# Context products in float32 on two 64-column halves, and maxima in pairs on two 64-row halves

## The reference

```python
q_big = einsum('bshk,hkq->bshq', hidden_q @ Wq.T, w_kc_q)   # then rope, width 192
kv_r  = rope(kv_c)                                          # [b, 1444, 64]
q_r, k_r = einsum(q_big, W_qr), einsum(kv_r, W_kr)          # width 64
attn  = softmax(einsum('bhsr,bhlr->bhsl', q_r, k_r))
ctx_c = einsum('bhsl,bld->bhsd', attn, kv_r)                # then w_kc_kv and Wo
```

## Time and profile before

| | |
|---|---|
| median of 3 runs | 2277.09 us (2274.82 to 2286.96) |
| the profiled execution | 2283.25 us, span 2281.4 us |
| weights and queries | to 305 us |
| first attention | 308 to 1373 us |
| the rest | to the end |
| mean granted clock of TensorE | 0.905 of full speed |

### The profile page before, as it was taken

The page is one execution under the profiler, slowest core; times in us unless marked ns, Lnnn a source line. Parts: engine busy times, 40 slices in busy tenths (PEclk is TensorE's granted clock), DMA queues, the critical chain, the costliest instruction groups (busy, mean ns, idle before and its releaser), DMA issues. The chain is left out here.

```text
span 2281.4 us, 38538 instructions
## 1 busy us (share of the span) xinstructions
PE 1857.9 (81%) x10550; PEld 1632.6 (72%) x10550; DVE 1492.1 (65%) x2799; ACT 1220.5 (53%) x2996; POOL 1117.1 (49%) x961
## 2 busy tenths in 40 slices
PE   4999958999999999999999973499993689837870
PEld 3677736888888888888888963499993466626870
DVE  4677777777777777767776433377774466656763
ACT  2111115777777767767777851366661266515650
POOL 0455528888788888878888852300004100014005
PEclk9999967999999999999999985699996599958985
DMA  5522251111111111111110002455542100026654
GB/s 159 197 58 57 55 176 55 63 63 63 45 54 63 64 31 63 63 64 63 63 54 11 16 8 78 140 197 196 204 165 58 34 1 0 0 77 196 198 164 113
DMA packets 115748, 195.76 MB, mean 86 GB/s; under 512 B 48213, under 2 KB 94265, under 8 KB 110161
## 3 DMA queue, kind: packets, MB, share of 16 engines
q1 hardware_dynamic: 107409, 180.88, 24.6%
q0 software_dynamic: 8192, 13.15, 2.0%
HBM read 147.01 MB, written 46.63 MB: 85 GB/s over the span
## 5 line engine op out<-in xcount | busy, mean ns | idle before, releaser
L501 POOL TENSOR_TENSOR EL<-E,EH 128x400 fp32r<-128x400 f32 x688 | 833.4, 1239 | 158.5 <-ACT EH L733 154.0
L599 DVE TENSOR_REDUCE PM<-bank 128x1 f32<-128x482 f32 (+1 forms) x624 | 397.2, 650 | 185.9 <-PE bank L578 182.9
L742 ACT ACTIVATE E<-bank 128x400 f32<-128x400 f32 x768 | 386.4, 503 | 212.8 <-PE bank L793 153.2
L733 ACT ACTIVATE EH<-E 128x400 fp32r<-128x400 f32 x768 | 407.0, 532 | 0.0
L175 PE MATMUL bank<-EH,KVH 128*128 128x400 f32 x768 | 283.1, 369 | 19.8 <-POOL EL L501 18.5
L578 PE MATMUL bank<-KH,QS 128*128 128x482 f32 (+1 forms) x624 | 250.9, 414 | 53.9 <-DVE KVL L549 27.6
L1248 POOL DMA_INDIRECT m_back<-rows_out,m_slots x64 | 64.8, 1013 | 450.8 <-DMA rows_out<-m_ys 421.2
L792 PE MATMUL bank<-QS,KH 128*128 128x400 f32 x768 | 272.1, 354 | 14.9 <-issue 9.1
L793 PE MATMUL bank<-QB,KB 66*128 66x400 f32 x768 | 269.1, 350 | 0.0
L175 PE MATMUL bank<-EH,KVL 128*128 128x400 f32 x768 | 265.7, 346 | 0.0
L175 PE MATMUL bank<-EL,KVH 128*128 128x400 f32 x768 | 265.5, 346 | 0.0
(11 more groups left out here) (244 smaller groups left out, 3983.3 us busy)
## 6 DMA issues: line engine op xcount, KB each, us to landing
m_stage_u<-in_m_up SPq DMA_DIRECT2D x20, 1392.0 KB
raw<-in_ctx_T SPq DMA_DIRECT2D x16, 1444.0 KB, 6.1
m_xg<-rows_in SPq DMA_DIRECT2D x55, 256.0 KB, 4.1
rows_out<-m_ys SPq DMA_DIRECT2D x55, 256.0 KB, 3.7
m_stage_d<-in_m_down SPq DMA_DIRECT2D x20, 696.0 KB
queries<-q_out SPq DMA_DIRECT2D x64, 200.0 KB, 2.4
QS<-queries SPq DMA_DIRECT2D x16, 800.0 KB, 6.1
rows_in<-zeros SPq DMA_DIRECT2D x5, 1792.0 KB
```

Source lines behind the costliest of these rows:

```text
L501: ops.tensor_tensor(EL[:, n % PB, :], E[:, n % EB, :], as_f32(EH[:, n % PB, :]), ALU.subtract).then_inc(sem, 1)
L599: nc.vector.tensor_reduce(PM[:, f:f + 1], psum[F0 + f % f_banks(b)][:, 0:KW[f % KC]], AX.X, ALU.max).then_inc(red_done, 1)
L733: nc.scalar.activation(EH[:, n % PB, :], E[:, n % EB, :], ACT.Copy).then_inc(hi_done, 1)
L742: nc.scalar.activation(E[:, n % EB, :], psum[S0 + n % SB][:, 0:CH], ACT.Exp).then_inc(exp_done, 1)
```

## The change

The context products use the exponentials in float32 as they are. EH, EL, KVH, KVL and the steps that make them go; the rotated keys are kept once, as KV (float32, `[P, KT, DC]`). A batch has 24 steps, each with one key tile and two score tiles of 4 heads: the even heads of eight (o = 0) and the odd ones (o = 1). The two context products of a step write rows 0 to 63 and 64 to 127 of one bank, CTX.

The row sums leave TensorE's long sums: VectorE adds the even heads' exponentials up in a PSUM bank, ACC (`sum_even`), GpSimd the odd heads' in EA (`sum_odd`), and after 12 steps a product with `ones` per half adds over the partitions (`sums`). GpSimd also takes the first ten parts of the rotation from VectorE.

QB now has 128 rows: the maximum in rows 1 and 2, a row for the padded keys in row 0, the high part of the queries in rows 64 to 127. The maximum uses the high part of the queries alone. Its 39 pieces go in 20 pairs, the even piece with rows 0 to 63 of QS and KH, the odd one with rows 64 to 127 of QB and KH, into two banks that one reduction reads. The list of TensorE has 12 double steps: pair, scores of two steps, pair, context products of two earlier steps.

In `latent_queries` M2 has 64 columns. Two heads' narrow products write the halves of one bank, and high and low part are made for both heads at once into `out_h` and `out_l`, which SyncE sends in four transfers. At the start VectorE clears more: QB over rows 64 to 127 (pad) and 0 to 63, KB over rows 0 to 63, then rows of ones and PAD one by one, and the first query loads wait for that. SR and RS take two transfers each.

Added lines and some unchanged ones (what is removed is in the kernel above):

```diff
...
+                    nc.tensor.matmul(psum[2 + h % 2][0:HALF, half * DC:(half + 1) * DC],
+                                     wqr[:, h, half * HALF:(half + 1) * HALF], wkr[:, h, :], start=True, stop=True)
...
+                def narrow(c, j):
+                    pe.wait_ge(rot_done, c * H + (BUFS + 2 * j + 2))
+                    pe.wait_ge(lo_done, c * HP + (j + 1))
                     for half in range(2):
+                        for o in range(2):
+                            h = 2 * j + o
+                            last = nc.tensor.matmul(psum[4 + j % 2][o * DC:(o + 1) * DC, 0:CH], M2[:, half, h, :],
+                                                    rot[:, h % TURNS, half, :], start=half == 0, stop=half == 1)
...
+    NS = 2 * KT
+    KC, KW = 3, 482
+    KAT = [0, 481, SK - KW]
     NF = QT * KC
+    NP = -(-NF // 2)
     SB, FB = 3, 2
+    EB = 8
...
+    PAD = -1.0e30
+    S0, F0, CTX, ACC, MISC = 0, 3, 5, 6, 7
+    SUM_AT, SUM0_AT, OUT_AT, TURN_AT = 2, 8, 9, 10
+    RECIP_AT, CT_AT = 9, 14
+    ROT_AT = (3, 4, 5, 6, 8, 9, 10, 11, 13, 14)
+    HI_AT, LO_AT = (17, 18), (18, 20)
+    ROT = 11
...
+        KV = [fixed(ctx, nc, f"KV{r}", [P, KT, DC]) for r in range(BUFS)]
...
+        R = fixed(ctx, nc, "R", [P, EB, 2, CH])
+        EA = fixed(ctx, nc, "EA", [P, CH])
+        ES = fixed(ctx, nc, "ES", [P, 2, 2, CH])
+        ones = fixed(ctx, nc, "ones", [P, DC])
...
+        def max_pair(pe, b, i):
             r = b_mod(b)
+            depth = 2 if b is FIRST else 1
+            if i >= depth:
+                pe.wait_ge(red_done, b_val(b) * NP + (i - depth + 1))
             elif b is not FIRST:
+                pe.wait_ge(red_done, b_val(b) * NP)
+            for f in pieces(i):
+                t, j = divmod(f, KC)
+                rows = slice((f % 2) * DC, (f % 2 + 1) * DC)
+                high = QB if f % 2 else QS
+                last = nc.tensor.matmul(psum[f_bank(b, i) + f % 2][:, 0:KW], high[r][rows, t * P:(t + 1) * P],
+                                        KH[r][rows, KAT[j]:KAT[j] + KW], start=True, stop=True)
+            last.then_inc(f_ready, 1)
...
+        def reduce_pair(v, b, i):
+            v.wait_ge(f_ready, b_val(b) * NP + (i + 1))
+            if i == 0 and b is not FIRST:
                 v.wait_ge(nm_ready, b_val(b))
+            k, n = f_bank(b, i), len(pieces(i))
+            nc.vector.tensor_reduce(PM[:, 2 * i:2 * i + n], banks[:, k:k + n, 0:KW], AX.X, ALU.max).then_inc(red_done, 1)
...
+        def sum_even(v, b, n):
+            p, t = divmod(n, KT)
+            v.wait_ge(exp_done, b_val(b) * 2 * NS + (2 * n + 1 + SB))
+            v.wait_ge(even_sum, b_val(b) * NS + (EB + n))
+            acc = psum[ACC][:, 0:CH]
+            if t == 0:
+                ins = nc.vector.tensor_copy(acc, tile_of(n, 0))
+            elif t < KT - 1:
+                ins = nc.vector.tensor_tensor(acc, acc, tile_of(n, 0), ALU.add)
+            else:
+                if b is not FIRST:
+                    v.wait_ge(sum_done, b_val(b) * 2 + (p - 1))
+                ins = nc.vector.tensor_tensor(ES[:, p, 0, :], acc, tile_of(n, 0), ALU.add)
+            ins.then_inc(even_sum, 1)
+        def sum_odd(pool, b, n):
+            p, t = divmod(n, KT)
+            if t == 0:
+                return
+            pool.wait_ge(exp_done, b_val(b) * 2 * NS + (2 * n + 2 + SB))
+            done = b_val(b) * 2 * ADDS + (p * ADDS + t - 1)
+            if t > 1 or p or b is not FIRST:
+                pool.wait_ge(odd_sum, done)
+            if t == KT - 1 and b is not FIRST:
+                pool.wait_ge(sum_done, b_val(b) * 2 + (p - 1))
+            first = tile_of(n - 1, 1) if t == 1 else EA[:]
+            out = ES[:, p, 1, :] if t == KT - 1 else EA[:]
+            nc.gpsimd.tensor_tensor(out, first, tile_of(n, 1), ALU.add).then_inc(odd_sum, 1)
...
+        def sums(pe, b, p):
+            pe.wait_ge(even_sum, b_val(b) * NS + (EB + KT * (p + 1)))
+            pe.wait_ge(odd_sum, b_val(b) * 2 * ADDS + ADDS * (p + 1))
+            if p == 0 and b is not FIRST:
+                pe.wait_ge(su_done, b_val(b) * 2)
+            for o in range(2):
+                last = nc.tensor.matmul(psum[MISC][o * DC:(o + 1) * DC, 0:CH], ones[:], ES[:, p, o, :], start=True, stop=True)
+            last.then_inc(sum_done, 1)
+        def sums_out(act, b, p):
+            act.wait_ge(sum_done, b_val(b) * 2 + (p + 1))
+            if b is not FIRST:
+                act.wait_ge(sr_in, b_val(b) * 32)
+            nc.scalar.activation(SU[:, p, :], psum[MISC][0:DC + 1, 0:CH], ACT.Copy).then_inc(su_done, 1)
+        def context_out(act, b, p):
+            act.wait_ge(av_done, b_val(b) * NS + (EB + KT * (p + 1)))
+            act.wait_ge(ct_ready, b_val(b) + 1)
+            nc.scalar.activation(CU[:, p, :], psum[CTX][:, 0:CH], ACT.Copy).then_inc(cu_done, 1)
...
+        def divide(v, b):
+            v.wait_ge(rs_in, b_val(b) * 32 + 32)
+            v.wait_ge(cu_done, b_val(b) * 2 + 3)
+            v.wait_ge(out_ready, b_val(b) + 1)
+            nc.vector.tensor_tensor(CT[:].rearrange("p h s -> p (h s)"), CU[:].rearrange("p g c -> p (g c)"),
+                                    RS[:].rearrange("p h s -> p (h s)"), ALU.mult).then_inc(ct_ready, 1)
...
+                        sum_odd(pool, b, n)
+                        if n in ROT_AT and has_keys:
+                            if n == ROT_AT[9]:
+                                pool.wait_ge(av_done, b_val(b) * NS + EB)
+                            rotate_part(pool, nc.gpsimd, b + 2, ROT_AT.index(n))
...
+                        if n == 0 and b is not FIRST:
+                            context_out(act, before(b), 1)
...
+                        if n == KT + 1:
+                            context_out(act, b, 0)
+                        if n == 2 * SUM0_AT + 1:
+                            sums_out(act, b, 0)
...
+                def scores(b, n):
+                    r = b_mod(b)
+                    p, t = divmod(n, KT)
+                    keys = slice(t * P, (t + 1) * P)
+                    for o in range(2):
+                        pe.wait_ge(exp_done, b_val(b) * 2 * NS + (2 * n + o + 1))
+                        out = psum[S0 + (2 * n + o) % SB][:, 0:CH].rearrange("p (j s) -> p j s", s=S)
+                        for lhs, rhs in ((KH, QS), (KB, QB)):
+                            heads = rhs[r][:, p * 2 * CH:(p + 1) * 2 * CH].rearrange("p (j o s) -> p o j s", o=2, s=S)
+                            last = nc.tensor.matmul(out, lhs[r][:, keys], heads[:, o], start=lhs is KH, stop=lhs is KB)
+                        last.then_inc(s_ready, 1)
...
                 def values(b, n):
+                    p, t = divmod(n, KT)
+                    pe.wait_ge(exp_done, b_val(b) * 2 * NS + (2 * n + 2 + SB))
                     if t == 0:
+                        pe.wait_ge(cu_done, b_val(b) * 2 + (p + 1))
+                    for o in range(2):
+                        last = nc.tensor.matmul(psum[CTX][o * DC:(o + 1) * DC, 0:CH], KV[b_mod(b)][:, t, :], tile_of(n, o),
+                                                start=t == 0, stop=t == KT - 1)
+                    last.then_inc(av_done, 1)
...
+                    for m in range(NS // 2):
+                        if has_next and m == 0:
                             pe.wait_ge(k_ready, b_val(b) + 2)
                             pe.wait_ge(q_in[b_mod(b + 1)], (b + 1).turn * 32 + 32)
+                        if has_next and 2 * m < NP:
+                            max_pair(pe, b + 1, 2 * m)
+                        if m == 0:
+                            if b is not FIRST:
+                                for n in range(NS - 2, NS):
+                                    values(before(b), n)
+                            pe.wait_ge(m_in, b_val(b) * 32 + 32)
+                        for n in (2 * m, 2 * m + 1):
+                            scores(b, n)
+                        if has_next and 2 * m + 1 < NP:
+                            max_pair(pe, b + 1, 2 * m + 1)
+                        if m == TURN_AT and has_next:
+                            pe.wait_ge(su_done, b_val(b) * 2 + 1)
                             if b is not FIRST:
                                 pe.wait_ge(res_done, b_val(b))
                             turn_max(pe, b + 1)
+                        for n in (2 * m - 2, 2 * m - 1):
+                            if n >= 0:
+                                values(b, n)
+                        if m == SUM_AT and b is not FIRST:
+                            sums(pe, before(b), 1)
+                        if m == SUM0_AT:
+                            sums(pe, b, 0)
+                        if m == OUT_AT and b is not FIRST:
+                            pe.wait_ge(su_done, b_val(b) * 2 + 1)
+                            project(pe, before(b))
...
+                        if has_next and n < NP:
+                            reduce_pair(v, b + 1, n)
+                        if n:
+                            sum_even(v, b, n - 1)
```

(31 more changed lines are left out.)

339 lines of the change are left out of this document (121 added, 218 removed).

## The result

The changed kernel takes 2208.75 us (median of 4 runs, 2204.17 to 2215.1) against 2280.26 (4 runs, 2274.82 to 2286.96): ratio 0.9687, 95% interval 0.9649 to 0.9725. Forecast were 2255 and a gain of 1%. The profiled execution fell from a span of 2281.4 to 2207.3 us, 74.1 less.

What follows compares the result with a forecast made beforehand. TensorE was taken to bound the batch stage, GpSimd close behind. Batches −8, queries −20, fold −2 and start +8 us made −22: 2261 us profiled, 2255 median; range 2180 to 2370, the sum's own 2230 to 2285.

Steps and rivals of the forecast that it cites:

- Context products: Values blocks on TensorE: eight records five deep, 1.69 us a block, 20.2 us a batch against 26.5 before.
- Maximum pieces: TensorE in each batch: 39 records become 20 pairs at 0.33 us each, 6.6 us a batch.
- Changes of arrangement: TensorE switching between product forms: 44 changes a batch at 0.16 us each, 7.0 us.
- Row sums: Products with ones on TensorE: two groups of depth three, 2.0 us a batch.
- The new wait at step 13: ScalarE's context copy waits for VectorE's divide; TensorE stands 3.3 us, costing 3.5 us a batch.
- a rival, at 0.20: Clock falls to half rate after the step 13 standstill: +42 us, 2300, slower; chance 0.20.
- Queries: Queries stage: 0.69 us less per pair of heads, 2 us more for chunk ends, −20 us in all.
- The fold: Weight fold with 64 columns instead of 128: at most 3 us saved, −2 taken.
- The start: Start of the attention: VectorE's clears take about 23 us against 11, +8 us.
- Cheaper on both: Rival: maximum pairs cost 0.22 us and changes of arrangement 0.11, giving 2190 us; chance 0.18.
- No overlap: Rival: the array's halves don't stream side by side, giving 2520 us; chance 0.12.
- changes at 0.35: Rival: each change of arrangement costs a record's whole 0.35 us, giving 2400 us; chance 0.10.

Runs made afterwards that it cites:

- Experiment 2: Changed kernel with both even-head context products of a double step listed first, then both odd ones: 2207.58 us.
- experiment 1: Changed kernel with the odd heads' context products from the second key tile on also sent to rows 0 to 63: 2425.33 us.
- experiment 4: Changed kernel with maximum pieces on all 128 rows, one after the other, 24 changes of arrangement a batch instead of 44: 2211.24 us.
- Experiment 3: Changed kernel with both maximum pieces of a pair on rows 0 to 63: 2329.64 us.
- Experiment 8: Changed kernel with three buffers for the context (CU) instead of one, divide still at step 14: 2152.76 us, ratio 0.9431 to the kernel before.
- experiment 6: Changed kernel with the divide two steps earlier and the clears of KB on GpSimd: 2188.58 us, ratio 0.9572 to the kernel before.
- experiment 7: Changed kernel with the second maximum pair of a double step moved between the scores of its two steps: 2242.18 us, ratio 0.9757 to the kernel before.

## Why the prediction was wrong

The sign and the mechanism were right: halves that stream side by side, paid for in changes of arrangement. The time lies in the stated range, but that was drawn wide for the rivals; the sum's own range, 2230 to 2285, was missed. The size was off by 46 us on the median (2255 against 2208.75). In the profiled execution 45 of the 52 us missed lie in the 13 steady batches, −3.74 each against −0.3.

**Context products: the step that failed.** I took five deep, 1.69 us a block, since "starts stay in order". Experiment 2 shows that they don't: each half works off its own records, so eight records are four deep, 4 × 0.337 = 1.35, and experiments 1 and 4 give the same. Over 12 blocks this is −4.1 a batch, the largest term. The Trainium skill (TensorEngine Tiling (Array Packing), Key Properties) has the rule that different tiles execute in parallel; experiments 1 and 2 agree with it (1.49 against 2.83 us), in either order of the list, which I had read too narrowly.

**Maximum pieces.** 0.33 a pair taken between ends of 0.22 and 0.44; it was the low end, 0.22: −2.2 a batch. Experiment 3 gives 0.45 without the overlap.

**Changes of arrangement.** 0.16 was right in kind and too cheap: 0.20, +1.8 a batch. It is a mean of the four changes of a double step.

**Row sums** took 1.36, not 2.0: two deep each, for the same reason as the values. −0.6.

**The new wait at step 13** is where I put it, with the size almost right for the wrong terms: 3.95 against 3.5. TensorE stood 2.35 instead of 3.3, because the divide took 0.98 and not 1.72 (GpSimd's last operation ended 0.13 us into it, then GpSimd stood still as well). But the clock fell, which I had as a rival, at 0.20, from somewhere between 2.8 and 3.7 us on. That reading of the rows was wrong. TensorE stands 2.29 to 2.37 us in 14 batches, and the clock falls behind it in 12 of them; in experiment 4 it stands 2.5 us each time and the clock falls in 7 of 14; before, it did not fall behind 2.8 us in one stretch, and the same trace had a third one, 2.50 us, which I left out, with the clock at 0.50 behind:

```profile
989.91 0.69 PE L792 MATMUL bank<-QS,KH 128*128 128x400 f32 x1 [2.50 <-issue]
```
```profile
990.00:991.00 1.00, 1.00 (x3) 0.99 (x4) 0.00 (x0) 0.00 (x0) 0.00 (x0) 0.50 0.08 16
```

So the length of the standstill alone doesn't decide. A fall cost about 1.6 us (1.4 in experiment 4), not 3. Experiment 8 shows the wait: without it, −3.95.

**Not foreseen**: 1.33 us in the first double step, where TensorE waits for the reduction of the first pair.

Together 61.5 − 4.1 − 2.2 + 1.8 − 0.6 + 0.45 + 1.3 = 58.1, measured 58.0. But for that reduction the other engines stayed hidden, as forecast.

**The stages.** Queries (−24.0, forecast −20) lose 0.76 us per pair of heads in the mean (200.7 / 31.5 = 6.37 for 7.13), chunk ends and all; I had 0.69 less, and +2 for the ends. The fold gave 3.4 instead of 2. The start was undersized: VectorE's clears run from 284.46 to 311.77, 27.3 us, where I had 23, and begin 11.6 us after the last rope product instead of 7.6: +16.6 for +8. It could be had back (experiment 6). The last batch has no next one, so no pairs, yet gained 8.6 us from its MH issue to its last exponential: I gave it −2 without working out its values and sums.

**The rivals.** Cheaper on both (2190) came nearest in time, by luck: only its pairs were right; the changes were dearer, and the values, which it left alone, carried the gain. No overlap is excluded by experiment 1, changes at 0.35 by experiments 4 and 7.

## What to carry to other kernels

Small products on separate halves of the array count by the deeper half, not by the list; what a change of arrangement costs (0.20 us here) is then the price to weigh them against, and pairs that save only 0.22 each, less two changes, are worth 0.4 to 0.5 us a batch in the rate. When an engine is freed, follow the one buffer that two batches share: here a copy queued in front of the exponentials cost 3.95 us in a plain batch, and two more buffers of 3.2 KB a partition bought back 2.6% of the time. Compare batches with the same granted clock: a fall is worth 1.4 us, as much as some of the edits above. A wait found in one kernel isn't the same wait in its neighbour: the same edit made the kernel before slower.

## What the runs showed of the hardware

- Float32 products on the two column halves stream side by side in either order of the list: eight records take 1.49 and 1.50 us to the next start, 2.83 on one half. A change of arrangement costs 0.20 us in the mean.
- A divide on VectorE with two operands in SBUF was held off through one GpSimd operation (2.41 us for 0.98) or through three in a row (5.13), and the GpSimd sum behind it was held off in its turn (1.79 for 1.05). The Trainium skill (SBUF — State Buffer, Who interferes with whom) says that whoever issues first has the shared ports for the whole instruction; the 2.41 and the 1.79 agree. The 5.13 goes beyond it: there the second and third operation, begun after the divide, went ahead of it. When that happens stays open.
- The granted clock fell to 0.50 after TensorE had stood 2.35 us (1.00 before, 0.50 over 677.3 to 680.7), in 12 of 14 batches, and behind 2.5 us in 7 of 14 in experiment 4, where the batch is 1.4 us longer for it; over a plain batch without that standstill it is 1.00 (experiment 8).
- Without the waits a double step is the same to 0.01 us from one to the next (697.38, 701.50, 705.62, 709.74 are the starts of its second pair in experiment 8).
